# A graph transformer layer: edge rows gathered straight into the items' places, without a ring, and SyncE in place of ScalarE for three kinds of loads and stores in each group

## What is computed

```
k, q, v = per-type linear maps of node_feat              # 6250 x 128 each
kt = einsum(k, relation_att)[edge_type, src]             # one row per edge
vt = einsum(v, relation_msg)[edge_type, src]
e  = (q[dst] * kt).sum(-1) * relation_pri[edge_type] * scale
m  = segment_max(e, dst);  ex = exp(e - m[dst])
a  = ex / segment_sum(ex, dst)[dst]
agg = segment_sum(a * vt, dst)
out = relu(per-type map of agg + node_feat @ loop_weight + bias)
x   = layernorm(x + out)
```

## Time and profile before

| | |
|---|---|
| median of 3 runs | 1298.87 us |
| lowest, highest | 1296.42, 1303.16 us |
| span of the profiled execution | 1757.2 us |
| granted TensorE clock, mean over the span | 0.783 of full |
| busy: PE / DVE / ACT / POOL | 1160.7 / 986.6 / 785.6 / 881.5 us |
| gathers (L1458) | 782 |
| copies from ring to kv (L1173) | 832 |

### The profile page before, as it was taken

The page is one execution under the profiler, slowest core; times in us unless marked ns, Lnnn a source line. Parts: engine busy times, 40 slices in busy tenths (PEclk is TensorE's granted clock), DMA queues, the critical chain, the costliest instruction groups (busy, mean ns, idle before and its releaser), DMA issues.

```text
span 1757.2 us, 31429 instructions
## 1 busy us (share of the span) xinstructions
PE 1160.7 (66%) x6730; PEld 962.9 (55%) x6730; DVE 986.6 (56%) x2832; ACT 785.6 (45%) x2217; POOL 881.5 (50%) x915
## 2 busy tenths in 40 slices
PE   8989875657556565566566655566565666656698
PEld 5445434656545554455455554565455565545587
DVE  7877463555445555445555554455554566545677
ACT  4667454444434434443344343443444354434324
POOL 2775354555555554545454545455545554545233
PEclk9999997777677767876777667766777687777699
DMA  8878754555555555545455555555555555555675
GB/s 261 323 289 316 284 172 140 157 148 158 152 159 153 157 151 151 149 141 151 150 163 148 158 152 154 148 160 164 151 162 154 154 168 148 155 150 162 187 242 194
DMA packets 225149, 309.08 MB, mean 176 GB/s; under 512 B 32423, under 2 KB 191119, under 8 KB 217781
## 3 DMA queue, kind: packets, MB, share of 16 engines
q1 hardware_dynamic: 159996, 188.75, 30.6%
q0 software_dynamic: 38880, 106.25, 23.4%
q10 hardware_dynamic: 26088, 12.08, 2.4%
HBM read 139.52 MB, written 58.78 MB: 113 GB/s over the span
## 4 chain that ended last, share of the span: by engine, by line
SPq 34%; issue 31%; PE 12%; DVE 9%; another core or an unknown queue 7%; DMA 2%; DVEq 2%; ACT 1%; POOL 1%; POOLq 0%; ACTq 0%
SPq L1173 27%; PE pb L1900 4%; SPq L1152 2%; PE pb L1923 2%; DVE agg L845 2%; SPq L481 2%; SPq L1170 2%; DVEq L814 2%; DMA kv<-ring 2%; PE pb L2084 1%; SPq L1168 1%; PE pb L2190 1%; PE pb L2028 1%; DVE kv L541 1%
## 5 line engine op out<-in xcount | busy, mean ns | idle before, releaser
L1458 POOL DMA_INDIRECT ring<-table,rows_idx x782 | 745.8, 954 | 736.6 <-SPq L1168 452.5
L2084 PE MATMUL pb<-work,onehot 128*128 128x136 f32 x1664 | 367.5, 358 | 214.1 <-DVE agg L845 152.8
L845 DVE TENSOR_TENSOR agg<-agg,pb 128x136 f32 x832 | 241.8, 291 | 459.9 <-remote 291.8
L2084 PEld LDWEIGHTS pb<-work,onehot 128*128 128x128 f32 x1664 | 307.0, 254 | 242.0 <-issue 210.9
L1650 ACT ACTIVATE work<-pb 128x512 f32<-128x512 f32 x208 | 124.0, 596 | 549.6 <-remote 376.2
L2028 PE MATMUL pb<-q_all,work 128*128 x1664 | 301.0, 340 | 1.3 <-issue 0.8
L2028 PEld LDWEIGHTS pb<-q_all,work 128*128 128x128 f32 x1664 | 280.6, 253 | 7.6 <-issue 4.9
L1637 ACT ACTIVATE work<-lane,neg_lane 128x128 f32<-128x128 f32 x800 | 253.3, 390 | 0.6
L2012 PE MATMUL pb<-ident,onehot 128*128 128x128 f32 x832 | 174.5, 347 | 115.6 <-issue 60.2
L2012 PEld LDWEIGHTS pb<-ident,onehot 128*128 128x128 f32 x832 | 125.4, 180 | 136.0 <-issue 71.3
L686 DVE TENSOR_TENSOR kv<-kv,pb 128x512 f32<-128x512 f32 x208 | 141.5, 680 | 96.6 <-issue 41.7
(11 more groups left out here) (239 smaller groups left out, 1237.2 us busy)
## 6 DMA issues: line engine op xcount, KB each, us to landing
kv<-ring SPq DMA_DIRECT2D x832, 128.0 KB
table<-kv SPq DMA_DIRECT2D x49, 1024.0 KB, 5.2
ring<-table,rows_idx POOLq DMA_INDIRECT x782
kv<-base_rows SPq DMA_DIRECT2D x7, 448.0 KB, 7.6
kv<-in_x_dram SPq DMA_DIRECT2D x8, 384.0 KB, 5.8
seg<-item_bias ACTq DMA_DIRECT2D x48, 64.0 KB
base_rows<-pair ACTq DMA_DIRECT2D x24, 128.0 KB
onehot<-coef_rows SPq DMA_DIRECT2D x3, 1024.0 KB, 5.5
```

What stands on the lines that cost most here:

```text
L845: v.tensor_tensor(a, a, PB[banks[i // 2 % len(banks)]][:, (i % 2) * 256:(i % 2) * 256 + W], ALU.add).then_inc(s_added, 1)
L1458: pool.indirect_dma_start(out=ring[:, o:o + 2 * D], out_offset=None, in_=table, in_offset=bass.IndirectOffsetOnAxis(ap=rows_idx[:, t:t + 1 ...
L2084: mm = t_.matmul(PB[banks[k % len(banks)]][:, u * 256:u * 256 + W], onehot[:, o:o + P], wv[:, b % WR, h * 2 + u, :], start=True, stop=True)
```

## The change

The ring goes. `rows_idx` becomes one column per item, so the tiles' row numbers are stored to a DRAM tensor `tile_src` (one plain DMA) and fetched in the items' order by 7 more indirect DMAs. POOL itself runs `bring(n)`: it waits until the place in `kv` is free and until batch n-2 has landed, then issues four gathers straight to the items' places, 832 in all. SP copies nothing; it issues the segment rows, the loads of x and the stores of base rows which ScalarE issued. The sums for the row numbers move from after the lanes into the loop that makes the pairs (L1365). The turns of the items' row numbers move from blocks 37 and 38 to blocks 38 and 39. Tile numbers are no longer sent to SP. The diff, cut to its core:

```diff
-        rows_idx = sb("rows_idx", [P, TILES], i32)
+        rows_idx = sb("rows_idx", [P, ITEMS], i32)
-        ring = sb("ring", [P, RING * 2 * D])
+        spare = sb("spare", [P, CN + 4 * NB * P])
...
-        ITEMS_AT = [34, 35, 37, 38]
+        ITEMS_AT = [34, 35, 38, 39]
...
@block.sync
-            sp.wait_ge(s_item_blocks, 48)
-            def bring(n):
...
-                for u in range(4):
-                    if u == 2 and n > 0:
-                        sp.wait_ge(s_gathered[(n - 1) // NBATCH % 2][(n - 1) % NBATCH], ...)
-                        sp.sem_inc(s_freed, 4)
-                    if u % 2 == 0:
-                        sp.wait_ge(s_landed, each[u + 1] & 1023)
-                        hold_apart(sp)
-                    sp.dma_start(kv[:, o:o + 2 * D], ring[:, ...]).then_inc(s_gathered[par][b], 16)
...
+            for g in range(1, GROUPS):
+                if g >= 2:
+                    load_pair(g - 1)
+                if g + 1 < GROUPS:
+                    segments(g + 1, (g + 1) % 2)
+                if g < GROUPS - 1:
+                    store_pair(g - 1)
+            sp.wait_ge(s_weighted, (GROUPS - 2) * NBATCH + 4)
+            sp.wait_ge(s_base_stored, 16 * (GROUPS - 4))
+            load_base(0)
+            sp.wait_ge(s_item_sums, (GROUPS - 2) * 2 * NBATCH + HALF * NB // 2)
+            load_coefs(0, 0, HALF)
+            store_pair(PAIRS - 1)
...
@block.gpsimd
+                if k == 1:
+                    pool.wait_ge(s_tile_more, 16 * 4)
+                    did(g_.tensor_copy(srcf, tsrc))
+                if k == 3:
+                    did(g_.tensor_copy(etf, tedge))
+                if k == 5:
+                    did(g_.tensor_scalar(srcf, srcf, float(T), None, ALU.mult))
+            did(g_.tensor_tensor(srcf, srcf, etf, ALU.add))
+            pool.dma_start(tile_src.rearrange("(p c) e -> p c e", c=TPR), ...).then_inc(s_tile_src, 16)
...
+            for k in range(IPR):
+                pool.indirect_dma_start(
+                    out=item_src[:, k, :], out_offset=None, in_=tile_src,
+                    in_offset=bass.IndirectOffsetOnAxis(ap=ic[:, 0, k:k + 1], axis=0)).then_inc(s_item_src, 16)
...
-            for t in range(REAL):
-                if t >= AHEAD:
-                    landed(t - AHEAD)
-                if t >= RING and t % 2 == 0:
-                    (done,) = nc.values_load_multi_w_load_instructions(next_start[0:1, ...], ...)[1]
-                    pool.wait_ge(s_freed, done & 1023)
-                    hold_apart(pool)
-                pool.indirect_dma_start(out=ring[:, o:o + 2 * D], ...).then_inc(s_tile[t % TSEMS], 16)
+            def bring(n):
+                g, b = n // NBATCH, n % NBATCH
+                par = g % 2
+                after(pool, s_weighted, g - 2, NBATCH, b + 1)
+                if n >= 2:
+                    pool.wait_ge(s_gathered[(n - 2) // NBATCH % 2][(n - 2) % NBATCH],
+                                 (n - 2) // (2 * NBATCH) * 64 + 64)
+                for u in range(4):
+                    o = (par * G + b * 4 + u) * 2 * D
+                    pool.indirect_dma_start(
+                        out=kv[:, o:o + 2 * D], out_offset=None, in_=table,
+                        in_offset=bass.IndirectOffsetOnAxis(
+                            ap=rows_idx[:, 4 * n + u:4 * n + u + 1], axis=0))\
+                        .then_inc(s_gathered[par][b], 16)
+            for n in range(GROUPS * NBATCH):
+                bring(n)
...
@block.scalar
-                    if prev and s == 1 and g >= 2:
-                        load_pair(g - 1)
...
-                        if not final:
-                            segments(g + 1, 1 - par)
...
-                    if prev and s == NBATCH - 1:
-                        store_pair(g - 1)
```

More of the change, by code:

```diff
@@ L86, in graph_transformer_layer @@
     WORK = 4 * P + 2 * 4 * P + WR * 4 * W + 2 * IH * P + 3 * IH * P
[L88 to L92, removed]
+    assert GROUPS * G < ITEMS
     table = nc.dram_tensor("table", [NP * T, 2 * D], f32, kind="Internal").ap()
@@ L217, in graph_transformer_layer @@
         tsrc, tedge = [a0.take(TPR * P, TROWS).bitcast(i32) for _ in range(2)]
+        srcf, etf = [a0.take(TPR * P, TROWS) for _ in range(2)]
         a0.at = at
@@ L242, in graph_transformer_layer @@
         y = [s3.take(CN) for _ in range(2)]
-        yo = (s3.take(CN), ring[:, 0:CN])
+        yo = (s3.take(CN), spare[:, 0:CN])
         an = [s3.take(CN) for _ in range(2)]
@@ L258, in graph_transformer_layer @@
         even_coefs = take_coefs(q3, CB)
-        ring_coefs = take_coefs(Space(ring, RING * 2 * D, at=CN), HALF)
+        spare_coefs = take_coefs(Space(spare, CN + 4 * NB * P, at=CN), HALF)
         first_coefs, odd_coefs = take_coefs(h3, HALF), take_coefs(h3, HALF)
@@ L1199, in _, with segments @@
                          x[0:2 * P, :].rearrange("(c p) d -> p c d", p=P)).then_inc(s_pair_loaded, 16)
[L1200 to L1211, removed]
+            def segments(g, par):
+                after(sp, s_maxima, g - 2, MX, MX_TOP)
+                seg3 = seg[:, par * (IH * P + 1):par * (IH * P + 1) + IH * P]\
+                    .rearrange("p (i e) -> p i e", i=IH)
+                for i in range(IH):
+                    sp.dma_start(seg3[:, i, :], item_bias[g * G + i * IL:g * G + i * IL + IL, :]
+                                 .rearrange("(a l) e -> a l e", a=1).broadcast_to([H, IL, P]))\
+                        .then_inc(s_segments[par], 16)
@@ new lines, in load_pair, with store_pair @@
+            def load_pair(j):
+                after(sp, s_base_stored, j, 16, 0)
+                if pair_of(j) == 2:
+                    sp.dma_start(pair[:, :].rearrange("p (c d) -> p c d", c=2),
+                                 x[bass.ds(j * (2 * P), 2 * P), :].rearrange("(c p) d -> p c d", p=P))\
+                        .then_inc(s_pair_loaded, 16)
+                else:
+                    sp.dma_start(pair[0:N - j * 2 * P, 0:D], x[j * 2 * P:N, :]).then_inc(s_pair_loaded, 16)
+            def store_pair(j):
+                after(sp, s_base_copied, j, 1, 1)
+                n = pair_of(j)
+                sp.dma_start(base_rows[bass.ds(j * (2 * P), n * P), :].rearrange("(c p) d -> p c d", p=P),
+                             pair[:, 0:n * D].rearrange("p (c d) -> p c d", c=n)).then_inc(s_base_stored, 16)
@@ L1442, in _ @@
             pool.wait_ge(s_items_copied, 2 * IPR)
-            def landed(t):
-                pool.wait_ge(s_tile[t % TSEMS], t // TSEMS * 16 + 16)
-                pool.sem_inc(s_landed, 1)
-            for t in range(REAL):
-                if t >= AHEAD:
-                    landed(t - AHEAD)
-                if t >= RING and t % 2 == 0:
-                    (done,) = nc.values_load_multi_w_load_instructions(
-                        next_start[0:1, t + 1 - RING:t + 2 - RING], engines=(pool.engine,), min_val=1,
-                        max_val=GROUPS * G, skip_runtime_bounds_check_because="counted from tiles")[1]
-                    pool.wait_ge(s_freed, done & 1023)
-                    hold_apart(pool)
-                o = t % RING * 2 * D
-                pool.indirect_dma_start(
-                    out=ring[:, o:o + 2 * D], out_offset=None, in_=table,
-                    in_offset=bass.IndirectOffsetOnAxis(ap=rows_idx[:, t:t + 1], axis=0))\
-                    .then_inc(s_tile[t % TSEMS], 16)
-            for t in range(REAL - AHEAD, REAL):
-                landed(t)
+            def bring(n):
[14 more added lines that the diff above has]
+                bring(n)
             def normed(ch):
@@ L1877, in turn_items @@
                 if i == 0:
[L1878 removed]
+                    pe.wait_ge(s_lanes, IPR)
+                if i == 2:
+                    pe.wait_ge(s_item_src, 16 * IPR)
                 bank_free()
[L1880 to L1881 removed]
+                each = (lanes, item_src)[a]
                 for k in range(k0, k1):
[L1883 to L1884 removed]
+                    t_.transpose(PB[0][:, (k - k0) * P:(k - k0 + 1) * P], each[:, k, :],
+                                 ident[:, :]).then_inc(s_items_turned, 1)
                 bank0.append((s_items_copied, a * IPR + k1))
```

87 lines of the change are left out of this document (17 added, 70 removed).

## The result

The changed kernel takes **1333.03 us** (median of 4 runs, 1331.07 to 1337.00) beside 1300.06 us for the kernel before (4 runs, 1296.42 to 1303.16). The ratio is 1.026, 95% interval 1.0227 to 1.0292: slower by 33 us. The forecast was 1365 us, 66 us slower, with a range from 1334. The direction was right, the size twice too large, and the time lies 1 us outside the range.

What follows compares the result with a forecast made beforehand. POOL's gathers, 1.258 us apart, were taken as the bound: 199.15 start + 1045.4 gathers + 16 stop + 2.9 landing + 93.5 end = 1357 us. The middle between that and 1373 gave 1365 us, range 1334 to 1390.

Steps and rivals of the forecast that it cites:

- the remainder: Whole kernel before: 16 us by which the one-engine sum, 1282.8 us, fell short of the median; half kept in the forecast.
- 832 copies fewer: SP in the groups: dropping the 128 KB ring copies gains 0, as SP's 30 us a group was below POOL.
- 50 gathers: POOL in the groups: 832 gathers instead of 782, at 1.258 us each, add 62.9 us.
- Less work ahead: POOL before the first weighing: only 64 items ahead instead of 64 + 16, so it stops 16 us; bounds 0 and 33.
- No copy behind the last gather: End of the gathers: the last batch is there after 2.9 us instead of 7.6, -4.7 us once.
- ScalarE's issues: Groups: taking loads and stores off ScalarE saves it 1.9 us a group, 0 for the time while POOL bounds.
- the preparation: Before the first gather: moved row-number sums, seven indirect DMAs and a later memset cost 0, covered by POOL's idle time.
- The slow stretches: First record's groups: stretches of slow small instructions taken as a recording cost, hardest on SP, absent from ordinary runs.
- VectorE at 30 us a group: Groups: VectorE, filled as in the fast stretches, needs about 30 us a group, below POOL's 37.8.
- Only the gathers count: Rival for the changed kernel: no stop and no remainder, 1341 to 1350 us; chance 0.15.
- The period is the record's: Rival listed first: gathers come closer in ordinary runs, below 1.208 us extra ones hide, about 1299 us or faster; chance 0.10.
- places freed too late: Rival in the groups: POOL stops 2 us in each of 24 groups, +48, about 1413 us; chance 0.10.

Runs made afterwards that it cites:

- a_no_repeats: Changed kernel without the 50 gathers of repeated tiles and padding, their places keeping old rows: 1274.96 us, ratio 0.9808 to the kernel before.
- b_no_copies: Kernel before without SP's ring copies from the third group on, which also drops its wait for their landing: 1279.01 us, ratio 0.9843.
- a_two_groups: Changed kernel gathering only for the first two groups, 64 items, later groups computing on those old rows: 1184.41 us, ratio 0.9118 to the kernel before.
- a_act_issues: Changed kernel with segment loads, pair loads and pair stores back on ScalarE: 1335.21 us, ratio 1.0279 to the kernel before.
- a_copies: Changed kernel with ScalarE issuing its loads and stores again and SP issuing 832 unread 128 KB copies: 1462.48 us, ratio 1.1262 to the kernel before.

## Why the prediction was half right

The forecast was 66 us slower, the runs show 33. The 33 us between the two are, to within rounding: a stop of 16 us that did not come; 13.4 us of held-up gathers and 8.7 us more behind the last gather, which went with the copies and their wait and stood at nothing, less the 8 us that halving the remainder had allowed for them; and 2.6 us at the start and the end.

- *What bounds the kernel before: wrong, and the main fault.* The text took POOL for the bound, because 782 periods and the ends came within 16 us of the median, and read SP as 3.76 us a batch. That row is from a stretch in which the DMA engines were busy for 0.31; there SP's wait for landings found a copy landed within 2.6 us of its issue (issued at 923.73, seen at 926.28). In the second record that share is 0.77 at 900 to 956 us, and the copies above land in 3.1 to 3.8 us. SP's loop was 4.66 to 4.99 us a batch, next to POOL's 4.55 to 5.02. A sum over one engine that misses by 1.2% did not prove that engine to be the bound; two near ties look the same from outside. The 1.2% was in part luck: with the true start, 192.19, and end, 91.9, the same sum is 1274 us, 25 us short, and 1274.96 us is what the changed kernel takes with those 782 gathers (a_no_repeats).
- *832 copies fewer, 0 because SP was below POOL: wrong.* They cost 20 us (b_no_copies), 13.4 in gathers held up and most of the rest behind the last gather. This term is the step that failed, together with the 16 us of remainder, of which the forecast kept half for the kernel after. The remainder was the copies' cost, and went with them.
- *50 gathers, +62.9 us: right.* They add 62.8 us between first and last gather, and 58 us when taken out. The period of 1.258 read from means is 1.2553.
- *Less work ahead, a stop of 16 us: wrong, and the largest single term of the miss.* There was none, the lower bound, though by a narrow margin: the first weighing started at 269.38 us, 2.1 us before the 65th gather, where the text put it at 296. It went by a first record whose 312.69 lay in slow stretches, and by 37 us for the ten steps from the first products to the first weighing. They take 29.4 us, as the eight steps of the first group take 16.8 and not 30. That is not for its rows having been there for long: with rows always there the later groups still take 33 us (a_two_groups). The first group has no group before it whose maxima, weighing and sums it would do. The bound of 33 us with "about 17" of it before is misread too: by its own rows the part before is 312.69 - 299.8, about 13.
- *No copy behind the last gather, -4.7 us: right in kind, too small.* 4.7 us remain of 18.1, so -13.4: the copies of the last two batches were also behind the last stage's loads in SP's queue.
- *The start.* 199.15 was the first record's; it is 192.19 and 191.26. Both sides had it, so it enters the time and not the difference.
- *The wait for batch n-2, ScalarE's issues, the preparation: 0, right.* No gather waits longer than 0.3 us; a_act_issues is the same within its interval; the memset of agg ends at 157.2 us, 34 us ahead of the first gather.
- *The slow stretches: right that ordinary runs have none, not shown why the record did.* The text laid them to recording, hardest on SP, and expected fewer once SP records little. The record after has none, but neither has the second record of the kernel before, with as many instructions as the first.
- *VectorE at 30 us a group:* 33.3 us for all consumers together, enough below 40.2 for the changed kernel.
- *The rivals.* "Only the gathers count", 1341 to 1350 at 0.15, had the right mechanism for the time after: no stop and no remainder. With measured values its sum is 191.3 + 1043.2 + 4.7 + 90.2 + 1.8 = 1331.2 us, the profiled execution's own time but for rounding, as it must be for pieces of one span; what shows the mechanism is that no gather waits. The point from which the first rival decides, 1.208 us, comes out at 1.207 from the text's own numbers. "The period is the record's" and "places freed too late" are both refuted by the timeline.
- *The Trainium skill.* By the "DVE blocks DMA" trap of the Trainium skill's page SBUF — State Buffer, GpSimd can't write descriptors while VectorE runs an operation in a two-port mode. In the changed kernel, with VectorE 74% busy, 832 gathers took 942 to 1358 ns, median 946, and landed in 2.7 to 3.7 us, so the trace shows no such stop; whether an operation of VectorE ran in that mode it does not say. By the Trainium skill's page DMA: Bandwidth & Descriptors (Anatomy of one DMA) a gather of 128 KB would land after an estimated 2.3 us. The median of the profile is 2.8, and the measurement decides.

## What to carry to other kernels

When a sum over one engine falls short of the measured time, look for a loop that goes through a landing: what an engine issues, how long the last of it takes to land while everything else is moving, and the wait that stands ahead of its next issue. Such a loop is not seen in the busy time of any engine; it shows in the chain as one kind of DMA that comes back once a batch, and one issue more inside it moved the whole kernel here by 138 us. Moving the wait behind the issues that do not need it cost nothing here, and did more than taking the stage out at the price of 50 gathers.

## What the runs showed of the hardware

- Gathers keep their pace beside other traffic: 1.2553 us apart at a DMA share of 0.42 (900 to 956 us, the changed kernel) and 1.254 us with 832 copies of 128 KB beside them, at a share of 0.73 (a_copies, 1150 to 1206 us). The copies do not: the last of four lands in 3.2 to 3.7 us beside gathers and the kernel's other work, in 2.1 us with nothing else moving (a_copies).
- One program gave records with spans of 1757.2 and 1296.0 us, its unrecorded runs taking 1300. A record far longer than the runs is worth taking again before a duration is read from it: here it put the first gather 7 us and the first weighing 41 us too late, and at its low traffic the copies landed sooner.
